# A rotation of weights worked into an attention and FFN kernel: two 64-row blocks a step in two corners of the TensorE array, half as many steps, and one PSUM bank moved from it to the scores

## The reference, cut to what matters

```python
# x: (2, 4096, 2048); 16 query heads of 128 share one key and one value head
x = layernorm(x + attn(x))        # causal, strictly below the diagonal
x = layernorm(x + ffn(x))
def ffn(x):                       # W1, W3: (8192, 2048)   W2: (2048, 8192)
    hidden = silu(x @ W1.T) * (x @ W3.T)
    hidden = fwht(hidden)         # Walsh-Hadamard over 8192, over sqrt(8192)
    return hidden @ W2.T
```

## Time and profile before

| what | us |
|---|---|
| three runs | 3311.98, 3313.93, 3318.64 |
| median | 3313.93 |
| the profiled execution | 3310.53 |
| its span on core 4 (the others 3297.4 to 3308.2) | 3308.9 |
| TensorE busy | 2635.1 (80%) |
| ScalarE busy | 753.4 (23%) |
| VectorE busy | 628.0 (19%) |
| mean granted TensorE clock, core 4 | 0.862 |

### The profile page before, as it was taken

How to read it: one execution, slowest core, us unless ns; L and a number is a source line. 1 busy time by engine, 2 the same in 40 slices (tenths; PEclk the granted TensorE clock), 3 DMA queues, 4 the chain that set the end, 5 groups by cost and what they waited for, 6 DMA issues and landing times.

```text
span 3308.9 us, 29218 instructions; the slowest of 8 cores (3297.4 to 3308.9 us)
## 1 busy us (share of the span) xinstructions
PE 2635.1 (80%) x10080; PEld 966.8 (29%) x10080; DVE 628.0 (19%) x888; ACT 753.4 (23%) x1387; POOL 150.0 (5%) x280
## 2 busy tenths in 40 slices
PE   3678666777778888868827999999999999894985
PEld 1223211111111222222213444444444444342432
DVE  1111255433332222212220000000000000002002
ACT  1222123344444444411162111111111110001001
POOL 1100000000000000000000000000000000000000
PEclk8779756677777788889958999999999999897997
DMA  6533411111110000033322122221222214444444
GB/s 188 157 114 102 146 51 45 45 32 33 32 32 26 26 26 26 18 110 102 92 93 89 65 70 70 71 70 64 70 70 70 71 51 134 143 152 148 149 146 146
DMA packets 96468, 276.77 MB, mean 84 GB/s; under 512 B 11716, under 2 KB 11844, under 8 KB 91976
## 3 DMA queue, kind: packets, MB, share of 16 engines
q0 software_dynamic: 34512, 139.48, 13.8%
q1 hardware_dynamic: 61816, 135.43, 12.2%
HBM read 224.54 MB, written 50.33 MB: 83 GB/s over the span
## 4 chain that ended last, share of the span: by engine, by line
PE 72%; DMA 11%; ACT 8%; DVE 5%; issue 4%; ACTq 0%; DVEq 0%; SPq 0%; POOL 0%; POOLq 0%
PE pb L175 72%; DMA W2P<-GA 8%; ACT GA L226 3%; DVE GA L230 2%; ACT GA L407 2%; DVE pb L404 1%; DMA GA<-X1S 1%; ACT GA L637 1%; DMA GA<-XBT 1%; DVE LNS L716 1%; ACT GA L551 1%; ACT GA L532 1%; ACT GA L539 0%; DVE GA L697 0%; DMA GA<-WOS 0%
## 5 line engine op out<-in xcount | busy, mean ns | idle before, releaser
L175 PE MATMUL pb<-GA 128*128 128x512 bf16 x8576 | 2156.6, 397 | 248.1 <-ACT GA L407 68.2
L175 PEld LDWEIGHTS pb<-GA 128*128 128x128 bf16 x8576 | 835.4, 100 | 1493.7 <-issue 673.0
L175 PE MATMUL pb<-GA,CB 128*1 128x512 bf16 (+2 forms) x1216 | 494.3, 432 | 305.3 <-DVE GA L230 221.6
L407 ACT ACTIVATE GA<-pb 128x512 bf16<-128x512 f32 x576 | 340.8, 597 | 538.9 <-PE pb L175 415.1
L175 PEld LDWEIGHTS pb<-GA,CB 128*1 128x1 bf16 (+2 forms) x1216 | 108.5, 94 | 679.6 <-issue 663.5
L637 ACT ACTIVATE GA<-pb 128x512 bf16<-128x512 f32 x128 | 69.6, 595 | 840.8 <-PE pb L175 840.7
L617 DVE TENSOR_TENSOR GA<-GA,pb 128x512 bf16<-128x512 f32 x128 | 82.3, 685 | 917.0 <-ACT GA L614 883.8
L230 DVE CAST GA<-pb 64x512 bf16<-64x512 f32 x256 | 164.4, 678 | 343.9 <-DMA W2P<-GA 182.9
L226 ACT CAST GA<-pb 64x512 bf16<-64x512 f32 x256 | 136.1, 578 | 264.6 <-PE pb L175 177.5
L404 DVE TENSOR_TENSOR pb<-pb,GA 128x512 f32<-128x512 f32 x128 | 89.0, 698 | 424.4 <-PE pb L175 421.6
L212 POOL DMA_DIRECT2D GA<-W2T x128 | 66.1, 516 | 1500.4 <-PE pb L175 1490.3
(11 more groups left out here) (43 smaller groups left out, 343.3 us busy)
## 6 DMA issues: line engine op xcount, KB each, us to landing
GA<-W2P SPq DMA_DIRECT2D x256, 256.0 KB, 2.6
GA<-W2T POOLq DMA_DIRECT2D x128, 256.0 KB, 3.6
W2P<-GA SPq DMA_DIRECT2D x128, 256.0 KB, 3.8
GA<-W1S POOLq DMA_DIRECT2D x64, 512.0 KB, 3.8
GA<-W3S POOLq DMA_DIRECT2D x64, 512.0 KB, 3.8
GA<-XBT POOLq DMA_DIRECT2D x8, 2048.0 KB, 13.3
GA<-WQS POOLq DMA_DIRECT2D x4, 2048.0 KB, 9.5
GA<-XOWN SPq DMA_DIRECT2D x1, 8192.0 KB, 30.4
```

The lines of the kernel that those rows point to most:

```text
L175: return e.matmul(out, lhsT, rhs, start=start, stop=stop, skip_group_check=True)
L407: texp = em.op("s", lambda e, qp=qp, slot=slot: e.activation(pbuf[slot], qp[:], AF.Exp, scale=SC), waits=_mx(dep, pbuf_rd[slot]))
```

## The change

A step takes two blocks of 64 rows instead of one, and there are 64 steps instead of 128. Of the two blocks, one lies in partitions 0 to 63 and the other in 64 to 127, for the load, for the matmul (with a second copy of H64 in partitions 64 to 127), in PSUM and in the staging buffer. Each quarter of a step has two matmuls, which are given the tile positions (0, 0) and (64, 64) of the array. Their results lie in the two halves of one bank, and one copy of 128x512 takes both. All four quarters of a step use bank 6. Bank 7 goes to the scores, which now go round banks 0, 1 and 7, and the exp goes round six buffers pbuf instead of four. The calls of the step stay where they were; since the count ends at 64, the last call that does something is the one after the sixteenth group of attention (k = 3, g = 3).

```diff
+        H64B = CB[64:128, 256:320]
...
-            if i >= 128:
+            if j >= 64:
                 return
...
+            tla = em.op("g", lambda e, wi=wi, j=j: e.dma_start(
+                wi[0:64, :], srcs[2 * j]),
+                waits=_mx(p0_state["wi_rd"][sl], tCB))
+            tl = em.op("g", lambda e, wi=wi, j=j: e.dma_start(
+                wi[64:128, :], srcs[2 * j + 1]),
+                waits=())
...
             for q4 in range(4):
-                bank = 6 + (q4 % 2)
-                ps = pb[bank]
+                ps = pb[6]
+                em.op("t", lambda e, ps=ps, wi=wi, q4=q4: MM(
+                    e, ps[0:64, :], H64, wi[0:64, q4 * 512:q4 * 512 + 512],
+                    True, True, tp=(0, 0)),
+                    waits=_mx(tla, tl, ps_tok[6]), inc=False)
                 tm = em.op("t", lambda e, ps=ps, wi=wi, q4=q4: MM(
-                    e, ps[0:64, :], H64, wi[0:64, q4 * 512:q4 * 512 + 512],
-                    True, True),
-                    waits=_mx(tl, ps_tok[bank]))
+                    e, ps[64:128, :], H64B, wi[64:128, q4 * 512:q4 * 512 + 512],
+                    True, True, tp=(64, 64)),
+                    waits=())
...
                     te = em.op("s", lambda e, ps=ps, q4=q4: e.copy(
-                        p0_st[0:64, q4 * 512:q4 * 512 + 512], ps[0:64, :]),
+                        p0_st[:, q4 * 512:q4 * 512 + 512], ps[:]),
                         waits=_mx(tm, p0_state["st_rd"]))
...
-            p0_state["st_rd"] = td
+            tda = em.op("y", lambda e, j=j, sA=sA: e.dma_start(dsts[2 * j], sA),
+                        waits=_mx(*evs))
+            td = em.op("y", lambda e, j=j, sB=sB: e.dma_start(dsts[2 * j + 1], sB),
+                       waits=())
+            p0_state["st_rd"] = _mx(tda, td)
...
-        pbuf_rd = [None] * 4
+        pbuf_rd = [None] * 6
...
-                        bank = sig_ctr % 2
-                        slot = sig_ctr % 4
+                        bank = QKB[sig_ctr % 3]
+                        slot = sig_ctr % 6
```

More of the change, by code:

```diff
@@ L170, in build_program, with MM @@
         H64 = CB[0:64, 256:320]
+        H64B = CB[64:128, 256:320]
         ONEC = CB[:, 320:321]
         ONER = CB[0:1, 320:448]
-        def MM(e, out, lhsT, rhs, start, stop):
+        def MM(e, out, lhsT, rhs, start, stop, tp=None):
+            if tp is None:
+                return e.matmul(out, lhsT, rhs, start=start, stop=stop,
+                                skip_group_check=True)
             return e.matmul(out, lhsT, rhs, start=start, stop=stop,
-                            skip_group_check=True)
+                            skip_group_check=True, tile_position=tp)
         tCB = em.op("y", lambda e: e.dma_start(CB[:], CONSTI[:]))
@@ L204, in p0_step @@
         def p0_step():
-            i = p0_state["i"]
-            if i >= 128:
+            j = p0_state["i"]
+            if j >= 64:
                 return
             p0_state["i"] += 1
-            sl = i % 2
+            sl = j % 2
             wi = p0_wi[sl]
-            src = W2T.rearrange("(a i) d -> i a d", i=128)[i]
-            tl = em.op("g", lambda e, wi=wi, src=src: e.dma_start(wi[0:64, :], src),
-                       waits=_mx(p0_state["wi_rd"][sl], tCB))
+            srcs = W2T.rearrange("(a i) d -> i a d", i=128)
+            tla = em.op("g", lambda e, wi=wi, j=j: e.dma_start(
[4 more added lines that the diff above has]
+                waits=())
             evs = []
@@ L216, in p0_step @@
             for q4 in range(4):
-                bank = 6 + (q4 % 2)
-                ps = pb[bank]
+                ps = pb[6]
[3 more added lines that the diff above has]
+                    waits=_mx(tla, tl, ps_tok[6]), inc=False)
                 tm = em.op("t", lambda e, ps=ps, wi=wi, q4=q4: MM(
-                    e, ps[0:64, :], H64, wi[0:64, q4 * 512:q4 * 512 + 512],
-                    True, True),
-                    waits=_mx(tl, ps_tok[bank]))
+                    e, ps[64:128, :], H64B, wi[64:128, q4 * 512:q4 * 512 + 512],
+                    True, True, tp=(64, 64)),
+                    waits=())
                 last_mm = tm
-                eng = "s" if (i % 2 == 0) else "v"
+                eng = "s" if (j % 2 == 0) else "v"
                 if eng == "s":
                     te = em.op("s", lambda e, ps=ps, q4=q4: e.copy(
-                        p0_st[0:64, q4 * 512:q4 * 512 + 512], ps[0:64, :]),
+                        p0_st[:, q4 * 512:q4 * 512 + 512], ps[:]),
                         waits=_mx(tm, p0_state["st_rd"]))
@@ L230, in p0_step @@
                     te = em.op("v", lambda e, ps=ps, q4=q4: e.tensor_copy(
-                        p0_st[0:64, q4 * 512:q4 * 512 + 512], ps[0:64, :]),
+                        p0_st[:, q4 * 512:q4 * 512 + 512], ps[:]),
                         waits=_mx(tm, p0_state["st_rd"]))
-                ps_tok[bank] = te
+                ps_tok[6] = te
                 evs.append(te)
             p0_state["wi_rd"][sl] = last_mm
[L236 to L239, removed]
-            p0_state["st_rd"] = td
+            dsts = W2P.rearrange("a t i d -> i t a d", i=128)
+            sA = p0_st[0:64, :].rearrange("p (a d) -> p a d", a=2)
+            sB = p0_st[64:128, :].rearrange("p (a d) -> p a d", a=2)
+            tda = em.op("y", lambda e, j=j, sA=sA: e.dma_start(dsts[2 * j], sA),
[3 more added lines that the diff above has]
+            p0_state["st_rd"] = _mx(tda, td)
+            p0_state["done"].append(tda)
             p0_state["done"].append(td)
@@ L352, in build_program @@
             waits=_mx(q_last_mm, wq_rd[0], wq_rd[1]))
-        qk_rd = {0: q_ps_rd[0], 1: q_ps_rd[1]}
+        qk_rd = {0: q_ps_rd[0], 1: q_ps_rd[1], 7: None}
+        QKB = (0, 1, 7)
         av_rd = {2: q_ps_rd[2], 3: q_ps_rd[3]}
@@ L498, in build_program @@
                 p0_step()
-        while p0_state["i"] < 128:
+        while p0_state["i"] < 64:
             p0_step()
@@ L567, in build_program @@
         ffn_ps_rd = [obank_rd[0], obank_rd[1], obank_rd[2], obank_rd[3],
-                     x1ps_rd[4], x1ps_rd[5], ps_tok[6], ps_tok[7]]
+                     x1ps_rd[4], x1ps_rd[5], ps_tok[6],
+                     _mx(qk_rd[7], ps_tok[7])]
         silu_rd = [None, None]
@@ L834, in _host_inputs @@
     CONST[0:64, 256:320] = hadamard(64).astype(bf)
+    CONST[64:128, 256:320] = hadamard(64).astype(bf)
     CONST[:, 320:448] = np.ones((128, 128), dtype=bf)
```

## The result

| | before | after |
|---|---|---|
| median of the runs, us | 3316.29 | 3330.01 |
| ratio after to before, 95% interval | | 1.0044 (1.0032 to 1.0055) |
| span of the profiled execution | 3308.9 | 3328.7 |

The change makes the kernel slower by 0.44%, some 15 us. The prediction was 3302.5, faster by 11 us, in a range of 3270 to 3338 and with 0.50 for faster. The time lies in the range and on the wrong side of no change.

A forecast was written before the change was run, and what follows sets the result against it. TensorE bounds the kernel, with the steps stalling it for some 430 us of the path. Terms: 137 (pairs) + 52 (queries) - 97 - 2 (attention) - 101 (output projection) = -11 us, so 3302.5 against 3313.9, range 3270 to 3338.

The forecast's parts named there:

- A pair that stays: the bank: 24 pairs of steps, keys/values and attention: one bank costs +1.88 us on ScalarE, +2.49 on VectorE, +0.2 for the clock.
- A pair that stays: the second matmul: Each quarter's second matmul in those 24 pairs: 0.05 us each, seven times a pair, +0.35 us a pair.
- Rival 3: The two matmuls of a quarter run one after the other: 65 us more, 3368 us; chance 0.12.
- A pair that stays: the writes: VectorE's first copy in 24 pairs waits for two writes: +0.8 us a pair, bounds 0 and 3.8.
- rival 2: The second write decides, at VectorE's first copy in 24 pairs: at 3.8 us, 72 more, 3374; chance 0.14.
- At nothing: Parts priced at zero: bank 7 and six buffers, POOL's 128 loads hidden behind matmuls, FFN and down matmuls untouched.
- The queries: 16 query steps, write hidden behind the next head's matmuls: +34 us for longer stalls, +18 for the clock, together +52.
- The groups without steps: Attention k = 4 to 7: 6.5 us saved in each of 15 groups, -97 us, and -2 for the sixteenth.
- rival 1: The clock stays up after the reciprocal's stall and in half the query steps: 35 us more gain, 3267; chance 0.15.
- The output projection: 32 steps go from the output projection: 235.4 us falls to 134.1, -101 us, bounds -98 and -104.
- At nothing: the third bank: Scores on a third bank and six exp buffers, in attention: worth nothing, since QK comes behind an AV that waited for exp.
- rival 4: The third score bank saves TensorE's 68 us of waits for exps in attention: 3235 if all went; chance 0.04.

The follow-up runs named there:

- the second experiment: The changed kernel with the scores on banks 0 and 1 and four exp buffers, steps still on bank 6, bank 7 unused: 3336.87 us, ratio 1.0047 to the kernel before.

## Why the prediction was wrong, step by step

**A pair that stays: the bank. Right.** The terms were +1.88, +0.2 and +2.49. The first copy to the write's issue took 4.48 (4.28 + 0.2 forecast), VectorE's first copy to QK 4.56 (4.45 + 0.15). Taking the bank away again gives 4.60 a pair and, in all, 169 us.

**A pair that stays: the second matmul. Right, nearly at nothing.** 0.40 us for the two where one takes 0.39; all 256 pairs of the trace start 2 to 4 ns apart. Rival 3 is out. By "TensorE: Matmul & The Clock Gate" of the Trainium skill the two start some 4 ns apart; the trace agrees. The sentence of "TensorEngine Tiling (Array Packing)" that different row tiles can't use one bank at the same time had no effect on the time here, where the two write different halves of the partitions; the measurement decides.

**A pair that stays: the writes. Here it failed.** "The second write costs between 0 ... and 3.8 ...; I take +0.8, since the transfer itself is what two can't share." The wait grew by 1.65 (5.55 against 3.90), past the 1.55 us from which rival 2 made the kernel slower by over 0.2%: 24 x 0.85 = 20 us more than forecast; in the table the stages with the pairs are 22 over. By the means of the five cases, a second write with no load in flight does cost 0.8 (3.93 against 3.11), the same beside one load (4.81 against 4.04), and the second load adds 0.9 that the sum did not have. That my 0.8 fits is partly luck: I had it from the time of the transfer, and 0.67 of it is the later issue of the second write. Rival 2 had the place and the price, and only part of the cause. The step that failed is the one that put the doubled loads under "At nothing": it asked only whether they come in time for their own matmuls, not what they are in flight with. A step's last matmul sets off its writes, through the copy, and the loads for the step after next, through the buffer, within 0.9 us, and it is the writes that VectorE waits for. Holding both loads brings the wait to 3.93 us and the kernel 63 us; holding one brings half of either. With the loads held, two writes take what one write beside one load took.

**The queries. Right in kind, 6.5 us short, and by two errors that partly cancel.** Most heads ran at the lower clock for a while, as expected: 8.2 to 9.6 us for 32 matmuls after both kinds of step, though one of 7.08 is there. "The write is hidden behind the next head's matmuls" was wrong in three heads:

```profile
283.35 0.57 SPq L250 DMA_DIRECT2D W2P<-GA  x1
...
284.05 0.55 POOL L333 DMA_DIRECT2D GA<-WQS  x1
...
297.31 0.58 ACT L237 CAST GA<-pb 128x512 bf16<-128x512 f32 x1 [4.83 <-DMA W2P<-GA]
```

In these heads a copy waited over 13 us from the issue of two writes with two block loads and a 2 MB load beside them (10.6 to 12.4 us on cores 0 and 5). Before had one such head of sixteen, where ScalarE waited 2.1 us and not 4.8. With the loads held the stage is 212.3 us long, 43 over the kernel before: the other terms of the 52 were some 9 us too high, and the late writes made 16.

**The groups without steps. Right.** The freed groups lose their wait for the write and gain one for the reciprocal:

```profile
1022.00 0.38 PE L177 MATMUL pb<-GA,CB 128*1 128x512 bf16 x1
...
1027.28 0.58 PE L177 MATMUL pb<-RB,CB 1*128 1x512 bf16 x1 [2.62 <-DVE RB L440]
...
1028.58 0.58 PE L177 MATMUL pb<-RB,CB 1*128 1x512 bf16 x1 [0.72 <-DVE RB L444]
1029.09 0.61 PE L177 MATMUL pb<-GA 128*128 128x512 bf16 x1
```

AV of the second tile is at R + 7.09, forecast 6.85, and the stage lost 97.8 us, forecast 99. The clock still falls after this wait (AV takes 0.61 us, where 0.39 is its time at the full clock), so rival 1 didn't come.

**The output projection. Right**: 134.6 us, forecast 134.1.

**At nothing: the third bank. Right**, shown by the second experiment; rival 4 is out.

Two sums of about 200 us cancelled, and an error of 0.9 us in one wait, 24 times, with 6 us in the queries, was enough for the sign. That the time still lies in the stated range is no merit of this term: the range had 0.5 us for it. The 0.8 was worked out from one queue's time on the DMA engines, as if the loads of the other queue did not use them too.

**Open.** Where in the DMA path the loads and writes hold each other up (the rings, the engines, the memory) was not tried. Why holding the loads brings so much less in the keys and values on two banks than on one is not known either.

## What to carry to other kernels

When a wait for a transfer is on the path, list everything that the same event sets off on the other queues; a prefetch that is early enough for its own reader can still be what makes the waited-for write late, and here one added wait held it back at no cost. When work is folded two for one, keep the double buffer that its round trip needs, and ask what the freed buffer's new owner waits for: here the program's order, not the bank. Before a stall is counted as saved, look for the next chain that it covered, and then move that chain's reader too.

## What the runs showed of the hardware

From the issue of the first 256 KB write to the start of the copy that waits for it, in attention, mean over pairs and cores: 3.11 us for one write alone, 4.04 beside one load of 256 KB, 3.93 for two writes, 4.81 with one load beside them, 5.74 with two. Beside a 2 MB load as well it was 10.6 to 14.0 us in the nine cases of three cores. The prediction had not seen that a single load costs a single write 0.8 to 0.9 us. Two 64x64 matmuls at tile positions (0, 0) and (64, 64), writing the two halves of one PSUM bank, started 2 to 4 ns apart and took 0.40 us for 512 columns where one took 0.39. With one bank a ScalarE copy of 128x512 started every 1.23 us; with two banks two copies ran into each other, 1.07 us for both.
